# Sums of exponentials joined by pairs on GpSimd, with the fourth tile of a plain sum added by a transfer

## What is computed

```
q, k, v = split(qkv);  q = rope(q); k = rope(k); k, v repeated for GROUP = 4 query heads
scores = q @ k.T / sqrt(32), masked above the diagonal
attn   = softmax(scores)            # exp(scores - max) / sum over the keys
out    = attn @ v
```

## Time and profile before

| | before |
|---|---|
| median of 3 runs | 3373.97 us (3373.56 to 3375.6) |
| profiled execution, its own time | 3371.2 us |
| span of the profiled execution | 3369.4 us |
| mean granted TensorE clock | 0.988 |
| PE busy | 3236.2 us (96%), 23824 products |
| PEld busy | 2288.1 us (68%) |
| DVE busy | 2391.3 us (71%) |
| ACT busy | 1423.1 us (42%) |
| POOL busy | 2245.7 us (67%) |

### The profile page before, as it was taken

How to read it: one execution, slowest core, us unless ns; L and a number is a source line. 1 busy time by engine, 2 the same in 40 slices (tenths; PEclk the granted TensorE clock), 3 DMA queues, 4 the chain that set the end, 5 groups by cost and what they waited for, 6 DMA issues and landing times. The chain is left out here.

```text
span 3369.4 us, 59196 instructions
## 1 busy us (share of the span) xinstructions
PE 3236.2 (96%) x23824; PEld 2288.1 (68%) x23824; DVE 2391.3 (71%) x4362; ACT 1423.1 (42%) x1679; POOL 2245.7 (67%) x1033
## 2 busy tenths in 40 slices
PE   1899999999999999999999999999999899999999
PEld 1778888846666666666666666666665688888887
DVE  3667777678888888888888888888883544444443
ACT  2222222235665666666566656656656200100110
POOL 3443330049999999999999999999998222332331
PEclk8999999989999999999999999999999999999999
DMA  9999994561221222122122212212221343433342
GB/s 240 242 253 230 233 234 147 147 198 42 68 63 38 63 65 59 43 73 63 43 58 66 54 43 69 57 43 55 60 57 35 120 95 96 93 86 100 92 90 63
DMA packets 248270, 335.04 MB, mean 99 GB/s; under 512 B 64371, under 2 KB 153715, under 8 KB 247995
## 3 DMA queue, kind: packets, MB, share of 16 engines
q1 hardware_dynamic: 229562, 264.13, 29.0%
q0 software_dynamic: 18432, 67.12, 9.3%
HBM read 227.73 MB, written 101.71 MB: 98 GB/s over the span
## 5 line engine op out<-in xcount | busy, mean ns | idle before, releaser
L932 ACT ACTIVATE probs<-st_ps 128x1024 f32<-128x1024 f32 (+1 forms) x1152 | 1066.5, 974 | 673.4 <-PE st_ps L1097 447.2
L984 DVE TENSOR_REDUCE mpart<-mx_ps 128x1 f32<-128x512 f32 (+2 forms) x1728 | 1092.0, 683 | 196.8 <-PE mx_ps L1058 132.3
L1058 PE MATMUL mx_ps<-k_max,qs 96*128 96x512 f32 (+3 forms) x2560 | 844.2, 399 | 9.8 <-DVE mpart L984 3.2
L1097 PE MATMUL st_ps<-qs,k_score 98*128 98x512 f32 (+1 forms) x2304 | 668.3, 390 | 0.0
L1058 PEld LDWEIGHTS mx_ps<-k_max,qs 96*128 96x128 f32 x2560 | 438.8, 190 | 315.5 <-DVE mpart L984 162.3
L901 POOL TENSOR_TENSOR sums<-sums,probs 128x1024 f32<-128x1024 f32 x252 | 607.4, 2410 | 20.5 <-ACT probs L932 0.8
L899 POOL TENSOR_TENSOR sums<-probs 128x1024 f32<-128x1024 f32 x252 | 601.4, 2386 | 17.4 <-ACT probs L932 12.9
L1113 PE MATMUL od_ps<-probs,vs 128*32 128x256 f32 (+1 forms) x9216 | 589.4, 373 | 1.4 <-ACT od_sb L939 1.4
L907 POOL TENSOR_TENSOR sums<-sums,probs 128x1024 f32<-128x1024 f32 (+1 forms) x252 | 531.4, 2109 | 19.8
L1097 PEld LDWEIGHTS st_ps<-qs,k_score 98*128 98x128 f32 x2304 | 421.0, 190 | 99.2 <-ACT probs L932 24.0
L1301 POOL TENSOR_TENSOR h<-h,bb 128x1024 f32<-128x1024 f32 x32 | 104.2, 3257 | 509.5 <-DVE xn_c L1375 509.5
(11 more groups left out here) (117 smaller groups left out, 3991.4 us busy)
## 6 DMA issues: line engine op xcount, KB each, us to landing
qs<-q_hi_scratch SPq DMA_DIRECT2D x128, 256.0 KB, 4.7
h_scratch<-hbuf SPq DMA_DIRECT2D x32, 512.0 KB, 4.4
q_hi_scratch<-rot_hi SPq DMA_DIRECT2D x64, 256.0 KB
q_lo_scratch<-rot_lo SPq DMA_DIRECT2D x64, 256.0 KB
qs<-q_lo_scratch SPq DMA_DIRECT2D x64, 256.0 KB, 5.9
o_scratch<-od_sb SPq DMA_DIRECT2D x128, 128.0 KB
o_in<-o_scratch SPq DMA_DIRECT2D x32, 512.0 KB, 4.9
o_in<-recip_scratch SPq DMA_DIRECT2D x128, 128.0 KB, 8.0
```

The lines of the kernel that those rows point to most:

```text
L932: nc.scalar.activation(probs[:, n % SLOTS, half, :, lo:QW], st_ps[:, half, :, lo:QW], ACT.Exp, scale=float(HD) ** -0.5).then_inc(exp_done, 1)
L984: nc.vector.tensor_reduce(mpart[:, rows, kc], scored, AX, ALU.max).then_inc(max_done, 1)
L1058: mm = nc.tensor.matmul(out[:, j], qs[c][0:K_ROWS, h, t * P:(t + 1) * P], k_max[0:K_ROWS, kc * CT:kc * CT + w], start=j == 0, stop=late or ...
L1097: mm = nc.tensor.matmul(out[:, :, lo:QW], k_score[0:M_ROW + 2, kt * P:(kt + 1) * P], qs[c // 2][0:M_ROW + 2, h:h + 2, at + lo:at + QW], st ...
```

## The change

GpSimd joins two neighbouring plain or diagonal sets of the same row of blocks into one sum, so that TensorE needs one denominators() step for both. joined_pairs() gives six pairs in a group: (4, 5), (7, 8), (10, 11), (14, 15), (16, 17) and (18, 19). After the second add of the second set, GpSimd waits for the first set's sum and adds it (one instruction more, on 128 x 1024). A first set of a pair has no denominators() step any more. In the last group, pairs with a set in DIRECT aren't joined, so (14, 15), (16, 17) and (18, 19) stay apart.

In all plain sets the last add L907 goes. In its place GpSimd issues a transfer that adds the fourth tile of exponentials to the sum in place (dma_start with accum_op=ALU.add, 128 rows of 4 KB). The transfer raises a semaphore of its own slot, sum_sent, by 16 when it has landed. Whoever waited for such a sum by sum_done now waits for sum_sent: TensorE in denominators(), ScalarE in exps(), GpSimd ahead of a join. A sum slot whose old sum went into a join needs no wait for TensorE.

```diff
+JOINED = joined_pairs()
+def carried(g, j):
+    return (j, j + 1) in JOINED and not unsummed(g, j) and not unsummed(g, j + 1)
+def sent_along(g, j):
+    return not unsummed(g, j) and len(SETS[j]) == 2 and all(STEPS[s][0] != STEPS[s][1] for s in SETS[j])
...
-                if q >= SUM_SLOTS:
+                if q >= SUM_SLOTS and not carried(*summed[q - SUM_SLOTS]):
                     pool.wait_ge(batch_done, last_use[q - SUM_SLOTS] + 1)
...
                 step.do(nc.gpsimd.tensor_tensor(at, at, probs_of(g, *wide[2], 0), ALU.add))
-                if diagonal:
-                    lo, last = P, (diagonal[0], 1)
-                else:
-                    lo, last = 0, wide[3]
+                if carried(g, j - 1):
+                    if (g, j - 1) in SENT:
+                        pool.wait_ge(sum_sent[SENT[g, j - 1][0]], SENT[g, j - 1][1])
+                    else:
+                        pool.wait_ge(sum_done, ENDED[g, j - 1])
+                    step.do(nc.gpsimd.tensor_tensor(at, at, sums[:, (q - 1) % SUM_SLOTS], ALU.add))
+                if sent_along(g, j):
+                    exp_waited(g, *wide[3])
+                    nc.gpsimd.dma_start(at, probs_of(g, *wide[3], 0), accum_op=ALU.add
+                                        ).then_inc(sum_sent[q % SUM_SLOTS], 16)
+                    return
+                lo, last = P, (diagonal[0], 1)
...
-                pe.wait_ge(sum_done, q + 1)
+                if (g, j) in SENT:
+                    pe.wait_ge(sum_sent[SENT[g, j][0]], SENT[g, j][1])
+                else:
+                    pe.wait_ge(sum_done, ENDED[g, j])
...
-                elif s == SETS[SET_OF[s]][-1]:
+                elif s == SETS[SET_OF[s]][-1] and not carried(g, SET_OF[s]):
                     mm = denominators(g, s)
```

More of the change, by code:

```diff
@@ L578, with joined_pairs @@
 DIRECT = [len(SETS) - k for k in (8, 6, 4, 2, 1)]
+def joined_pairs():
+    joined = set()
+    for c in range(QH):
+        pairs = [j for j, steps in enumerate(SETS) if STEPS[steps[0]][0] == c and len(steps) == 2]
+        odd = len(pairs) % 2
+        joined |= {(j, k) for j, k in zip(pairs[odd::2], pairs[odd + 1::2])}
+    return joined
+JOINED = joined_pairs()
 def unsummed(g, j):
@@ L588, in sums_made, with sums_counted @@
     return g * len(SETS) + sum(not unsummed(g, k) for k in range(j + 1))
+def carried(g, j):
+    return (j, j + 1) in JOINED and not unsummed(g, j) and not unsummed(g, j + 1)
+def sent_along(g, j):
+    return not unsummed(g, j) and len(SETS[j]) == 2 and all(STEPS[s][0] != STEPS[s][1] for s in SETS[j])
+def sums_counted():
+    ended, sent, last, by_slot = {}, {}, 0, [0] * SUM_SLOTS
+    for g in range(GROUPS):
+        for j in range(len(SETS)):
+            if sent_along(g, j):
+                slot = (sums_made(g, j) - 1) % SUM_SLOTS
+                by_slot[slot] += 1
+                sent[g, j] = (slot, 16 * by_slot[slot])
+            elif not unsummed(g, j):
+                last += 1
+                ended[g, j] = last
+    return ended, sent
+ENDED, SENT = sums_counted()
 LEAD, FIRST_LEAD = 17, 14
@@ L690, in part_b @@
         sum_step, sum_done, batch_done = sem("sum_step"), sem("sum_done"), sem("batch_done")
+        sum_sent = [sem(f"sum_sent{k}") for k in range(SUM_SLOTS)]
         od_copied = sem("od_copied")
@@ L929, in exps @@
                     act.wait_ge(batch_done, n - SLOTS + 1)
-                    if not unsummed(g_old, SET_OF[s_old]):
-                        act.wait_ge(sum_done, sums_made(g_old, SET_OF[s_old]))
+                    old = (g_old, SET_OF[s_old])
+                    if old in SENT:
+                        act.wait_ge(sum_sent[SENT[old][0]], SENT[old][1])
+                    elif old in ENDED:
+                        act.wait_ge(sum_done, ENDED[old])
                 nc.scalar.activation(probs[:, n % SLOTS, half, :, lo:QW], st_ps[:, half, :, lo:QW], ACT.Exp,
```

## The result

| | before | after |
|---|---|---|
| median | 3373.8 us (3373.5 to 3375.6) | 3594.7 us (3579.2 to 3597.9) |
| span of the profiled execution | 3369.4 us | 3596.1 us |
| mean granted TensorE clock | 0.988 | 0.957 |

A forecast was written before the change was run, and what follows sets the result against it. TensorE was taken to set the pace, with GpSimd just keeping it. Waits of 12.3 us less 2.6 saved, +9.7 in each of 15 groups, and +5.2 in the last made 3374 + 151 = 3525 us, range 3425 to 3600.

The forecast's parts named there:

- The sign and the mechanism: Whole kernel: slower, chance 0.90, because TensorE waits for joined sums that land too late; 151 us in all.
- 15 x 9.7: Fifteen groups, each 9.7 us longer: waits of 12.3 us less 2.6 saved; the last group adds 5.2.
- Pair by pair: TensorE's waits at the six joined sums, from GpSimd's work against TensorE's time between products: 12.3 us a group.
- GpSimd's issue, i: GpSimd's time to issue one adding transfer: 1.5 us, between 0.95 and 1.87, making its work 121.8 us a group.
- under 0.9 means a gain: Test of the forecast: if an issue takes 0.9 us or less, waits are small and the kernel gains.
- The landing, L: Time from a transfer's issue to its landing, in place of a 2.35 us add: 5.5 us, ends 3.7 and 7.
- The saving: TensorE's denominators() steps taken out: 0.43 us each, six a group 2.6 us, 93 steps 40 us in all.
- hidden rival: All transfers and joins hidden, so TensorE's saving of 40 us remains: 3334 us, chance 0.07.
- Net: One group: waits of 12.3 us less the 2.6 saved, so 9.7 us longer.
- if the period is over 130, L is longer: Test of the forecast: waits present but a group over 130 us would mean a landing longer than taken.
- The load of the DMA engines: Added DMA traffic, about half busy, costed at nothing; late maxima's rows would add up to 60 us.
- What was said would show it: Profile signs: denominators waits well over 100 us, period about 127, GpSimd over 0.85 busy, issues 1.2 to 1.6, 93 steps fewer.

The follow-up runs named there:

- e9: Kernel before without the six denominators() steps and their sets' last GpSimd adds, nothing joined or sent, part of the denominators missing: 3372.7 us, ratio 1.000.
- e3: Changed kernel with products by a tile of zeros ahead of TensorE's waits at sets 5, 11, 17 and 19: 3536.3 us, ratio 1.046.
- e1: Changed kernel without the joins, all 20 denominators() steps back, fourth tile of plain sets still added by transfer: 3507.2 us, ratio 1.038.
- e11: Changed kernel joining only (4,5), (14,15), sending only sets 3, 8, 13, 14, 17, VectorE's weight subtractions moved to steps 16 and 22: 3426.2 us, ratio 1.015.
- e12: Kernel before without six denominators() steps and their sets' last adds, VectorE's weight subtractions moved to steps 16 and 22: 3373.1 us, ratio 1.000.

## Why the prediction was right, and where it wasn't

The sign and the mechanism held: the joined sums are late at the pairs that the subtraction named. The size was 70 us short. In the profiled executions 226 us were lost: the waits less the saving, 15 x 9.3, some 72 us more in the same groups, nearly all of it the clock, and 14.1 in the last group, where 5.2 were forecast. That the first of these came out so near the forecast's 15 x 9.7 is in part luck: the waits were taken 1.6 us too large and the saving 1.2. By its own steps:

- **Pair by pair.** Forecast 2.8, 0.7, 3.0, 0.6, 1.9 and 3.3 us, in sum 12.3; measured 2.2, 0.2, 3.1, 0.5, 1.6 and 3.1, in sum 10.7. This was the best step, but not by its inputs. With the measured i of 1.1 the same subtractions give 2.6 at set 19 and 2.2 at set 11, where 3.1 were measured. There the landings are slower than elsewhere: 5.8 us (median) at set 19, and 6.3 at set 10, which goes into set 11. An issue taken too dear stood in for landings taken too cheap.
- **GpSimd's issue, i.** Taken 1.5, measured 1.1. With it GpSimd's work is 103.8 + 12 x 1.1 = 117 us of a group of 132: it isn't full, and it is the chain of add, join and landing at a pair that is late. The page shows the issue as 0.86; the "under 0.9 means a gain" was wrong, since the pairs wait at i = 1.1 as well.
- **The landing, L.** Taken 5.5; measured 4.5 at least, 4.8 in the median, and 9.8 at most. It was too dear where DMA traffic is low; where SyncE loads queries it was too cheap. The Trainium skill, DMA: Bandwidth & Descriptors, section Anatomy of one DMA, has 2.0 us + bytes / 436e3, an estimated 3.2 us here. No transfer of the 189 was that fast. At the packets, an adding row of 4 KB occupied an engine 0.33 us at its shortest and a plain one 0.16; that section of the Trainium skill has no term for the adding.
- **The saving.** Taken 0.43 x 6 = 2.6 us a group; measured 1.4 (0.3 to 0.4 at sets 4, 7, 14 and 16, 0 at 10 and 18). The earlier trace rows shows the length of a step of TensorE, but a step is worth its length only where TensorE sets the next start. At 18 the exponentials ended next. At 10 TensorE in e9 waited 0.34 us for exponentials and then for VectorE's maxima, and the step kept its length. The 40 us of the hidden rival weren't there either: with nothing added at all (e9) the gain is 0, as the 1.0 to 1.6 us that seven groups win are lost in the eight groups where the subtraction meets GpSimd's adds.
- **Net.** +9.7 forecast for a group, and 10.7 - 1.4 = 9.3 by the parts measured. With the clock held up (e3) it is 127.5 - 118.1 = 9.4, where most of the fills run inside the waits. The two ways agree.
- **The clock, costed at nothing because I never asked.** The earlier trace rows shows 1.00, and I took that as a fact of the stage, not of TensorE's being always busy. It is worth at least 58 us, most of the missing 70. What the two parts above leave of the 14.1 us of a group, 4.8, is what e3 wins, 4.7. The subtraction has a small share in it: step 12 of groups 2 to 9 is 0.9 us longer than in the other groups. The forecast's "if the period is over 130, L is longer" gave the wrong cause: the period is 132 and L is shorter than taken.
- **The load of the DMA engines.** Its share came out as costed (0.46). It was said to threaten the maxima's rows. It hit the sums instead: 5 us a group at sets 10 and 19 in e1, and, as far as the rows show it, some 9 us in the last group.
- **What was said would show it.** TensorE's waits well over 100 us by transfers: 107.8, so just over. 93 steps fewer: yes. GpSimd over 0.85 busy: 0.84. Period about 127: 132. An issue of 0.9 us or less would mean a gain: it took 0.86, and there was none.

Left open: the exact border between waits and clock in a group, since a wait ahead shortens the next one and the fills of e3 cost something where a wait was shorter. The three groups of e9 with one stretch of 3.4 us at the low clock, 1.5 us longer than their five neighbours, are a second price for it: at that rate the 13 us of a group in after would be an estimated 5.7, part of them inside the waits.

## What to carry to other kernels

Before costing a removed step by its own length, look at what else ends just before the next one starts, at that place: an engine that is busy 99% of a stage isn't the bound of every step in it, and here the removal alone was worth nothing as the kernel stood. An add moved from an engine to an accumulating transfer trades 2.4 us of the engine's time for about 1.1, and 4.5 us or more until the sum is there, so it suits sums whose user comes later than that and whose landing doesn't meet bulk loads. Where a change puts gaps into a TensorE that never stood still, count stretches at 1.2 GHz with it: here one came with most gaps of 2 us and more, and with a third of those between 1 and 2.

## What the runs showed of the hardware

- **Adding transfers.** 512 KB from SBUF to SBUF with accumulation, issued by GpSimd: GpSimd gives 0.30 us ahead and 0.86 for the issue, the next add starts 0.60 behind the issue's start; the first byte moves after 1.43 us, the last after 4.2, and it lands after 4.5 where it meets no bulk load (4.8 in the median of all 189). In e1 at set 19, beside SyncE's loads of 256 KB, the first byte came after 4.4 us and the last after 8.7 (medians).
- **The clock.** When a TensorE at 2.4 GHz stood 2 us or more for a sum, the granted clock went to 1.2 GHz for 3.4 or 6.8 us in 24 of 28 cases, sometimes while it still stood. In e9 one stretch of 3.4 us made a group 1.5 us longer. In the kernel before, with no such wait, this stage stayed at 2.4. Zero products in the waits kept it up and made the kernel 58 us faster.
- **VectorE beside GpSimd.** A subtraction of two SBUF tiles of 128 x 512 took 0.68 us at its shortest, 0.99 in the mean before, and 1.3 to 2.4 in the mean in the variants, though only e11 and e12 moved it; elsewhere only the times around it had moved. Where it started inside a GpSimd add, it ended 0.55 us behind that add (all 16 in e9).
